# Layer 0 experts of a two-layer transformer block: rows gathered per tile through an inverse permutation, results written to token order by indirect DMA

## The reference

```
def _L0_ffn_ref(x, Wr, br, W1, b1, W2, b2):
    xt = x.reshape(-1, Hd)
    logits = xt @ Wr + br
    probs = jax.nn.softmax(logits, axis=-1)
    gate = jnp.max(probs, axis=-1)
    idx = jnp.argmax(probs, axis=-1)
    h1 = jnp.maximum(jnp.einsum('th,ehf->etf', xt, W1) + b1[:, None, :], 0.0)
    ye = jnp.einsum('etf,efh->eth', h1, W2) + b2[:, None, :]
    onehot = jax.nn.one_hot(idx, n_exp, dtype=xt.dtype)
    y = jnp.einsum('te,eth->th', onehot, ye) * gate[:, None]
    return y.reshape(B, S, Hd)

x = x + gb * _L0_ffn_ref(h, ...)      # h: layernorm of x, scaled and shifted per batch
h = _layernorm(x, axis=-1) * (1 + ca) + sa
x = x + ga * _L1_attn_ref(h, ...)
```

## Time and profile before

| | us |
|---|---|
| median of 3 runs | 1377.56 |
| lowest, highest | 1376.34, 1378.93 |
| the profiled execution, whole | 1384.38 |
| its span, from the first instruction to the last | 1382.1 |

### The profile page before, as it was taken

One profiled execution on the slowest core, in us unless ns is written; L12 is line 12 of the kernel. 1 busy time (PEld: TensorE's weight loads), 2 busy tenths in 40 slices (PEclk: granted clock), 3 DMA queues, 4 the chain that ended last, 5 costly groups with the idle time before them and its releaser, 6 DMA issues. The chain is left out here.

```text
span 1382.1 us, 26590 instructions
## 1 busy us (share of the span) xinstructions
PE 1098.9 (80%) x8456; PEld 492.4 (36%) x8457; DVE 986.3 (71%) x1542; ACT 733.8 (53%) x1423; POOL 251.1 (18%) x358
## 2 busy tenths in 40 slices
PE   4876309974775599999999999999999987788876
PEld 3765207751332022222222222222222246546644
DVE  6776604433876699999999999999999628644535
ACT  3231102320222078889889888888898852412321
POOL 2101350005644000000000000000000031071053
PEclk8985659995777589999999999999999998589999
DMA  6800011221548501111011111100111002012322
GB/s 207 285 1 1 21 55 39 61 72 38 128 110 167 105 2 30 30 29 28 3 28 28 28 28 28 28 16 14 28 28 30 3 1 115 0 46 66 110 72 73
DMA packets 101963, 75.47 MB, mean 55 GB/s; under 512 B 41720, under 2 KB 86136, under 8 KB 101136
## 3 DMA queue, kind: packets, MB, share of 16 engines
q1 hardware_dynamic: 97808, 66.32, 20.2%
q0 software_dynamic: 4096, 8.40, 2.0%
HBM read 41.48 MB, written 33.16 MB: 54 GB/s over the span
## 5 line engine op out<-in xcount | busy, mean ns | idle before, releaser
L1477 DVE TENSOR_REDUCE mx<-at_psA 128x1 f32<-128x1024 f32 x512 | 592.2, 1216 | 53.5 <-PE at_psA L1401 50.4
L1537 ACT ACTIVATE at_pt<-at_psS 128x512 f32<-128x512 f32 x1024 | 554.0, 595 | 108.7 <-PE at_psS L1421 97.5
L1401 PE MATMUL at_psA<-K,Q 48*128 48x512 bf16 x1024 | 320.9, 394 | 33.6 <-PEq L1075 16.3
L1434 PE MATMUL at_acc<-at_pt,V 128*32 128x256 f32 x4096 | 328.4, 392 | 13.0 <-ACT attn L1529 12.6
L1421 PE MATMUL at_psS<-Q,K 51*128 51x512 bf16 x1024 | 310.3, 383 | 1.4 <-ACT at_pt L1537 0.5
L1434 PEld LDWEIGHTS at_acc<-at_pt,V 128*32 128x32 f32 x4096 | 81.5, 108 | 216.8 <-issue 114.3
L1401 PEld LDWEIGHTS at_psA<-K,Q 48*128 48x128 bf16 x1024 | 60.7, 94 | 258.1 <-DVE mx L1477 181.2
L1511 POOL TENSOR_TENSOR mr<-zeros,mx 128x16 f32<-128x16 f32 x32 | 7.1, 223 | 602.0 <-DVE mx L1477 602.0
L730 POOL DMA_INDIRECT sorted<-h_l,slot x64 | 63.2, 987 | 98.5 <-DVE slot L700 79.6
L952 DVE TENSOR_TENSOR e_h<-e_ps,b 128x512 f32<-128x512 f32 x40 | 27.7, 691 | 68.0 <-PE e_ps L917 68.0
L1421 PEld LDWEIGHTS at_psS<-Q,K 51*128 51x128 bf16 x1024 | 61.0, 94 | 17.5 <-ACT at_pt L1537 13.5
(11 more groups left out here) (234 smaller groups left out, 1405.7 us busy)
## 6 DMA issues: line engine op xcount, KB each, us to landing
Q<-q_rows SPq DMA_DIRECT2D x32, 192.0 KB, 4.3
K<-k_rows SPq DMA_DIRECT2D x32, 192.0 KB, 4.8
e_rows<-sorted SPq DMA_DIRECT2D x22, 256.0 KB, 2.9
result<-e_y SPq DMA_DIRECT2D x22, 256.0 KB, 2.3
w<-in_w SPq DMA_DIRECT2D x2, 2048.0 KB, 11.4
k_rows<-p_part SPq DMA_DIRECT2D x8, 512.0 KB, 4.2
sorted<-zeros SPq DMA_DIRECT2D x1, 3072.0 KB, 22.2
q_rows<-p_part SPq DMA_DIRECT2D x4, 768.0 KB, 3.5
```

What stands on the lines that cost most here:

```text
L1401: mm = pe.matmul(psA[t][:, c * 512:(c + 1) * 512], Q[slot][rows, h // 2, q0:q0 + P], K[slot][rows, h // 2, c * 512:(c + 1) * 512], start=T ...
L1434: mm = pe.matmul(acc[VW * h:VW * (h + 1), cols], V[slot][:, kc, h * (HD + 1):h * (HD + 1) + VW], pt[s % 2][:, h, cols], start=(kc == 0 and ...
L1477: dve.tensor_reduce(mx[s // KC % 2][:, h, qt:qt + 1], psA[t][:], AX.X, ALU.max).then_inc(a_max, 1)
L1537: act.activation(pt[s % 2][:, HEADS[j], :], psS[bank(s, j)][:], ACT.Exp, scale=INV_SCALE).then_inc(exp_done, 1)
```

## The change

**No scatter, no zero fill.** `sorted[0]` and its fill are gone, and so is `result[0]`. During routing SP stores `M.h` batch by batch, in token order, to a DRAM tensor `hrows0`.

**Inverse permutation.** After `slot`, DVE splits the slot number into its tile (`hif`) and its lane (`lof`), and makes one-hot tables of both: `ohhi` (32 x 40 values per partition), times the partition number and times the token tile's number plus one (`who`), and `ohlo` (32 x 128, in two halves of 16 tiles). PE adds up 32 bf16 matmuls of `ohlo` with `who` (128 x 80) in the PSUM bank `psL`. DVE makes of it, for each of the 40 tiles, the row to read (`gidx`) and the row to write (`sidx`; slots without a token go to rows of their own behind the 4096).

**Tiles on demand.** POOL gathers the first 8 tiles at the end of routing and waits for them. In the experts phase POOL gathers group g (four tiles) when PE has transposed group g - 2, then puts the four tiles of y of group g - 2, each when it is ready, by indirect DMA to `yrows0` in token order; the last eight are put at the end. SP has nothing to do there.

**Projections.** SP loads `M.h` from `yrows0` with four plain DMAs of 512 KB, ahead of the rope table. POOL's 32 gathers are gone.

Four small constants are loaded more, the number of semaphores that last over phases is 32 in place of 5, and layer 1 is unchanged.

More of the change, by code:

```diff
@@ L579, in phase_route @@
         dve_rt, half_done = n.sem("dve_rt"), n.sem("half_done")
+        if l == 0:
+            h_stored, lo_ready, hi_ready = n.sem("h_stored"), n.sem("lo_ready"), n.sem("hi_ready")
+            inv_mm, idx_ready = n.sem("inv_mm"), n.sem("idx_ready")
+            hii, hif, lof = n.sb("hii", [P, NT], I32), n.sb("hif", [P, NT]), n.sb("lof", [P, NT])
+            ohlo, ohhi = n.sb("ohlo", [P, NT, P], BF16), n.sb("ohhi", [P, NT, NS], BF16)
+            who = n.sb("who", [P, NT, 2, NS], BF16)
+            tile_row, pad_row = n.sb("tile_row", [P, NS]), n.sb("pad_row", [P, NS])
         psT = [n.ps(f"psT{i}", [P, 512]) for i in range(2)]
@@ L875, in phase_experts0 @@
     with Names(nc, "e0_") as n:
-        loaded = [n.sem(f"loaded{i}") for i in range(2)]
         x_T, xT_ready, mm1_done, h1_ready = n.sem("x_T"), n.sem("xT_ready"), n.sem("mm1_done"), n.sem("h1_ready")
         h1_T, h1T_ready, mm2_done, y_ready = n.sem("h1_T"), n.sem("h1T_ready"), n.sem("mm2_done"), n.sem("y_ready")
-        stored = [n.sem(f"stored{i}") for i in range(2)]
-        rows = [n.sb(f"rows{i}", [P, GT, P]) for i in range(2)]
+        put = [n.sem(f"put{i}") for i in range(U)]
+        rows = M.rows
         xT = [n.sb(f"xT{i}", [P, GT, P]) for i in range(2)]
@@ L888, in phase_experts0, with _ @@
         psY = [n.ps(f"psY{i}", [P, 512]) for i in range(2)]
-        src = M.sorted[0].rearrange("(s p) e -> p s e", p=P)
-        dst = M.result[0].rearrange("(s p) e -> p s e", p=P)
         with nc.Block() as block:
-            @block.sync
-            def _(sp):
-                move_tiles(sp, NS0, src, dst, rows, y, loaded, stored, x_T, y_ready)
+            @block.gpsimd
+            def _(pool):
+                def put_tile(k):
[12 more added lines that the diff above has]
+                    put_tile(k)
+                for slot in range(U):
+                    pool.wait_ge(put[slot], 16 * (NS0 // U))
             @block.tensor
@@ L904, in step @@
                     if S.has(k) and r % GT == 0:
-                        pe.wait_ge(loaded[gs], i * 16 + 16)
+                        for t in range(GT):
+                            pe.wait_ge(M.got[gs * GT + t], i * 16 + 16)
                         if after(k, U):
@@ L1111, in _ @@
             def _(pool):
[L1112 to L1117, removed]
                 def rstd(b):
@@ L1159, in combine @@
                     tiles = range(b * TB, (b + 1) * TB)
[L1160 removed]
+                    dve.wait_ge(gathered[b], 16)
                     for i in tiles:
@@ L1895, in declare_experts0 @@
     M.b10, M.b20 = n.sb("b10", [P, E0, F0]), n.sb("b20", [P, E0, P])
+    M.rows = [n.sb(f"rows{i}", [P, GT, P]) for i in range(2)]
 def declare_experts1(M, n):
```

48 lines of the change are left out of this document (34 added, 14 removed).

## The result

The changed kernel takes 1387.43 us (median of 5 runs, 1385.94 to 1390.71), the kernel before beside it 1378.93 us (5 runs, 1376.34 to 1382.13). The ratio is 1.0048, 95% interval 1.0026 to 1.0070: slower by half a per cent, where 1360.8 us and a range of 1351 to 1371 were forecast. The profiled execution took 1385.94 (span 1384.1).

What follows compares the result with a forecast made beforehand. POOL's serial scatters were taken to bound routing, PE the experts; terms -19.8 + 5.0 + 2.5 - 1.6 - 2.9 = -16.8 us, from the median 1377.56 to 1360.8 us, range 1351 to 1371.

Steps and rivals of the forecast that it cites:

- Rival C: Experts stage: POOL's issues cost 1.78 us each, making the change slower, 1388.0 us in all; chance 0.05.
- Routing: Slot to PE's first expert transposes: tables, matmuls and eight gathers replace 32 scatters and a load; -19.8 us.
- Experts: Experts stage: POOL's eight indirect DMAs per group take 10.1 us against PE's 9.2, so POOL bounds it; +5.0 us.
- A: Experts stage: POOL is no bound, two DMAs per tile cost less than 1.17 us each; 1355.8 us, chance 0.08.
- B: Experts stage: every POOL issue costs 1.42 us, the price beside DVE; 1369.0 us, chance 0.12.
- End of the experts: Last y to the next phase's first DMA: the last put starts 0.45 us after y, 5.3 follow; +2.5 us.
- Start of the projections: DVE's first combine waits for the rope table behind 2 MB of h, 12.4 us instead of 14.0; -1.6 us.
- Rest of the projections: Without POOL's gathers ahead of the splitting, DVE waits less for rstd in batches 1 and 2; -2.9 us.
- At nothing: Zero fill, four constants, SP's stores of h and clearing more semaphores: nothing gained or lost.

Runs made afterwards that it cites:

- a3: Changed kernel with the first instruction of TensorE's layer 1 attention loop at number 100 of a 256-instruction block; 1391.85 us, 1.0054 of the kernel before.
- a1: Changed kernel with the first instruction of TensorE's layer 1 attention loop at the start (0) of a 256-instruction block; 1367.63 us, 0.9885 of the kernel before.
- b4: Changed kernel, loop head at 0, every second gather of the experts stage left out from group 2 on, with PE's wait for it; 1361.9 us in one run.
- b2: Changed kernel, loop head at 0, DVE's wait for the rope table moved behind the first normalising; 1360.79 us, 0.9842 of the kernel before.
- c2: Changed kernel with TensorE's attention loop head at instruction 48, its last 11 instructions in an eighth block; 1404.12 us in one run.
- b1: Changed kernel, loop head at 0, one more GpSimd drain ahead of the last eight puts of the experts; 1367.53 us, 0.9891 of the kernel before.

## Why the prediction was wrong

The step that failed is the sentence on all that comes behind the projections, "left as it is, and I take it as moved". Its code is left as it is; its place in the blocks of TensorE's instruction memory is not, and the attention took 17.5 us more, which is more than the 13.7 gained ahead of it. No rival held it either. Rival C's 1388.0 is close to the measured 1387.43 by luck: the slow issues from which it comes did not occur. The page of before had the row that it hung on, 32 instruction packets, and its trace has none of them between 640 and 1020 us, in the loop; nothing in the prediction asks what keeps it so.

The profiled pair differs by only 2.0 us where the medians differ by 8.5: the changed kernel's profile is its fastest run, that of before lies 5.5 above its median. So 17.5 may be low for a usual run; a3's attention took 22 more than a1's.

With the loop's place equal the sum was nearly right. With the head at 0 in both kernels, the ratios are 0.9885 and 1.0001, a gain of 16.0 us of 1382.2 where 16.8 were forecast (by the two intervals 12 to 20); the stretches of these two runs up to the attention give 13.4. With the head at 100 in both it is 1.0054 against 1.0131, 11 us. By its own steps, from the profiled pair:

1. **Routing, -19.8**: 182.14 - 205.44 = -23.3, from the stretch alone -24.0, outside the bound of -22.6. The tables were near their price: the four took 1.49, 0.55, 1.48 and 4.49. The matmuls behind the second half took 1.25, not 3.5, so that gidx stood 10.6 behind slot and not 13.3. From the last gather's start to PE passed 4.1 and not 5.8: the 5.3 taken from the earlier trace rows held a drain for 32 indirect DMAs, and here there were eight.
2. **Experts, +5.0**: +7.9. The last gather started 82.9 behind the first transposes, where the forecast's sum has 83.2, with the DMAs 1.27 apart from tile 3's put on. But PE could use its data 4.57 after its start and not 2.7 (the gathers from 250 us on landed in 2.5 to 4.3 us, those between 200 and 230 in 2.4 to 3.2; no run shows why), and from there to the last y passed 17.2 instead of 15.8. b4 confirms the bound. Of rivals A, B and C (1.17, 1.42 and 1.78 an issue) none came: in this stage every put and gather was busy for 0.94 to 1.00 us, with DVE at work beside them. Only the first two gathers of routing were dearer, 1.39 and 1.14; the six behind them took 0.94 or 0.95 though DVE worked on. The rule weighed for B and C (the Trainium skill, DMA: Bandwidth & Descriptors, SWDGE vs HWDGE vs iDMA: DVE in its two-port mode locks GpSimd out) did not show in the issues of this stage. SP had issued two DMAs a group, not the eight that rival C takes from it.
3. **End of the experts, +2.5**: +5.9. The last put started 0.54 after y, nearly as forecast (0.45), but the next phase 8.7 behind it, not 5.3. It is the same mistake as in step 1 with the other sign: a duration taken whole, of which a part goes with the number of DMAs.
4. **Start of the projections, -1.6**: -2.0; the rope released DVE at 12.0, forecast 12.4. By the Trainium skill (DMA: Bandwidth & Descriptors, Anatomy of one DMA), as the prediction works it out, it would have been 9.2, an estimate from a fit to DMAs of GpSimd; the trace, with SP's, disagrees. The prediction's bound of some 9 less without the rope in the way is near b2's 7.8.
5. **Rest of the projections, -2.9**: -2.4. DVE waits 0.72 for rstd behind combines 1 and 2, as behind combine 3 in the earlier trace rows.
6. **At nothing**: the front ended at 107.1 to 108.5 us in three profiles of the kernel before and at 106.8 to 111.6 in ten with the change; the zero fill, the constants and the cleared semaphores gained and cost nothing that these show.

The sum at the start of the attention is -13.7 for a forecast of -16.8: steps 1 and 3 err by 3.5 each in opposite senses, step 2 by 3.

## What to carry to other kernels

Before a change adds instructions ahead of a long loop, count the loop's instructions on its engine and where it begins: a loop of nearly seven blocks ran without a fetch by the luck of its place, and an edit ahead of it can then move the time by more than the edit is worth. Look at the instruction packets of the page first when an untouched stage changes; fix the head's place or put a hint at the loop's top, and compare versions with that fixed. And split a duration between two phases into its parts before it is used for another number of DMAs.

## What the runs showed of the hardware

- TensorE ran a loop of seven blocks (1,755 instructions) for turn after turn with no fetch; in eight it was fetched again in each turn, 7 to 9 packets of 16 KB, and the whole attention took 16 to 34 us more. With a hint for the branch back, eight blocks ran with no fetch either.
- A pause of 2.4 to 4.5 us at the branch can be followed by a stretch at the lower clock (0.60 of full from 637 to 642 us in the changed kernel; 41 us in all in c2).
- GpSimd's drain at a phase's end takes time for each indirect DMA issued since its last drain: 0.70 us for 8, 2.67 for 32, 4.63 for 56, 5.94 for 72, that is 82 ns each. b1's early one, begun behind a put, took 8.88 for 64 and doesn't lie on that line. These are the drain's rows in the kernel before (routing of both layers) and in b4:

```profile
L607 POOLq DRAIN  x2: 2670/2671/2672, 199.6 to 1254.8; - x2
```

```profile
L952 POOLq DRAIN  x1: 4628/4628/4628, 280.6 to 280.6; - x1
```

- 16 bf16 matmuls of 128 x 80 took 1.22 to 1.25 us, 0.08 each, where the earlier trace rows have 3.58 for 16 small f32 passes.
